# Four graph layers on one core: degrees from one-hot sources ahead of the counts, and the first layer's matmuls beside them

## The reference, cut to what matters

```python
edge_index = jnp.stack([src, dst])
x = _layernorm(x + _L0_gnn_ref(x, edge_index, L0_gnn_W, L0_gnn_b), axis=-1)
...
    # _L0_gnn_ref; ei holds the edges and one more loop at each node
    row, col = (ei[0], ei[1])
    h = jnp.einsum('nd,od->no', x, W) + b
    deg = jnp.zeros((num_nodes,), dtype=h.dtype).at[row].add(1.0)
    deg_inv_sqrt = deg ** (-0.5)
    norm = deg_inv_sqrt[row] * deg_inv_sqrt[col]
    msg = norm[:, None] * h[col]
    out = jax.ops.segment_sum(msg, row, num_segments=num_nodes)
```

## Time and profile before

| | us |
|---|---|
| median of 3 runs | 3709.14 (3701.06 to 3714.17) |
| profiled execution, its own time | 3702.35 |
| its span, first to last instruction | 3700.6 |
| TensorE matmul busy | 3465.3 (94%) |
| VectorE busy | 2024.3 (55%) |
| GpSimd busy | 1349.8 (36%) |
| ScalarE busy | 941.1 (25%) |

### The profile page before, as it was taken

One profiled execution on the slowest core, in us unless ns is written; L12 is line 12 of the kernel. 1 busy time (PEld: TensorE's weight loads), 2 busy tenths in 40 slices (PEclk: granted clock), 3 DMA queues, 4 the chain that ended last, 5 costly groups with the idle time before them and its releaser, 6 DMA issues.

```text
span 3700.6 us, 55568 instructions
## 1 busy us (share of the span) xinstructions
PE 3465.3 (94%) x22684; PEld 2647.9 (72%) x22684; DVE 2024.3 (55%) x4409; ACT 941.1 (25%) x1367; POOL 1349.8 (36%) x1093
## 2 busy tenths in 40 slices
PE   5899678999999999989989989899999999999998
PEld 4666457899899899934434478677777777777797
DVE  7877475432433454364443367777676644444477
ACT  0112123111211312222212266342222122222224
POOL 3777525566456467757777211300000000000021
PEclk8899889999999999989999989999999999999999
DMA  8799884543643455445554355552442322222233
GB/s 288 191 267 290 291 267 112 160 122 81 181 122 99 144 167 173 157 144 163 162 163 136 114 215 177 188 187 98 147 138 79 128 80 81 80 81 66 72 104 107
DMA packets 268704, 557.26 MB, mean 151 GB/s; under 512 B 94954, under 2 KB 118143, under 8 KB 266430
## 3 DMA queue, kind: packets, MB, share of 16 engines
q1 hardware_dynamic: 124504, 384.00, 29.7%
q10 hardware_dynamic: 64520, 116.89, 8.9%
q0 software_dynamic: 79424, 52.83, 8.8%
HBM read 370.13 MB, written 183.44 MB: 150 GB/s over the span
## 4 chain that ended last, share of the span: by engine, by line
PE 76%; DVE 9%; DMA 6%; POOL 5%; issue 3%; ACT 1%; SPq 0%; ACTq 0%; POOLq 0%; DVEq 0%
PE ps L430 52%; PE ps L791 11%; DMA EM<-ee,adr 3%; PE ps L520 3%; PE ps L435 2%; POOL gr L2435 2%; DVE eqj L954 2%; POOL EM L2425 2%; DVE eqj L951 1%; PE ps L676 1%; PE ps L677 1%; PE ps L678 1%; POOL gl L2435 1%; DMA slab<-T 1%; PE ps L444 1%
## 5 line engine op out<-in xcount | busy, mean ns | idle before, releaser
L430 PE MATMUL ps<-a,yy 128*128 128x384 f16 (+5 forms) x3200 | 430.5, 297 | 6.2 <-DVE yy L1627 5.3
L430 PE MATMUL ps<-wb,xh 128*128 128x256 f16 (+1 forms) x2560 | 427.3, 274 | 8.6 <-DVE xl L1199 5.4
L791 PE MATMUL ps<-mh,whl 128*128 128x384 f16 (+5 forms) x2048 | 427.2, 302 | 8.5 <-DVE ml L1774 7.5
L2475 POOL TENSOR_TENSOR graw<-graw,rsb 128x1280 f32<-128x1280 f32 (+1 forms) x2 | 5.7, 2851 | 1090.9 <-DMA graw<-GD 1090.9
L430 PEld LDWEIGHTS ps<-a,yy 128*128 128x128 f16 (+1 forms) x3200 | 312.0, 98 | 124.0 <-DVE yy L1627 5.6
L2386 POOL DMA_INDIRECT TR<-cnt,adr x167 | 268.1, 1605 | 352.5 <-DMA TR<-cnt,adr 325.6
L430 PE MATMUL ps<-wb,xl 128*128 128x256 f16 (+1 forms) x1280 | 350.1, 273 | 0.0
L676 PE MATMUL ps<-sl,x 128*128 128x512 f16 (+1 forms) x800 | 307.5, 384 | 36.9 <-ACT ue L2108 30.3
L2386 POOL DMA_INDIRECT T<-cnt,adr x167 | 265.2, 1588 | 139.9 <-DMA T<-cnt,adr 81.1
L791 PE MATMUL ps<-ml,whl 128*128 128x384 f16 (+5 forms) x1024 | 307.7, 300 | 0.0
L677 PE MATMUL ps<-sl,x 128*128 128x512 f16 (+1 forms) x800 | 307.5, 384 | 0.0
(11 more groups left out here) (346 smaller groups left out, 6908.3 us busy)
## 6 DMA issues: line engine op xcount, KB each, us to landing
TR<-zero_w SPq DMA_DIRECT2D x80, 625.0 KB, 5.3
EM<-neg ACTq DMA_DIRECT2D x40, 625.0 KB
wraw<-in_L_gnn_weight SPq DMA_DIRECT2D x48, 512.0 KB, 3.3
UD<-ue ACTq DMA_DIRECT2D x90, 256.0 KB, 3.1
uu<-UD SPq DMA_DIRECT2D x45, 512.0 KB, 6.1
ar<-TR SPq DMA_DIRECT2D x72, 320.0 KB
eb<-EM SPq DMA_DIRECT2D x9, 2500.0 KB, 9.0
ar<-TR SPq DMA_DIRECT2D x72, 305.0 KB
```

What stands on the lines that cost most here:

```text
L430: i = pe.matmul(ap, l, r, start=(q == 0), stop=(q == len(pairs) - 1))
L791: ins = pe.matmul(ps[:, 0:cn], l, r, start=(q == 0), stop=(q == len(pairs) - 1))
```

## The change

The degrees no longer come from the finished counts. Sources are split on VectorE into 32 a + b, compared with a row 0 to 39 (and 0 to 31) into fp16 one-hot tables `oha` and `ohb`, and 167 matmuls of 32x40 add their products: the number of edges at source 32 a + b. One more matmul spreads these over partitions, and a mask picks each node's. Row sums and diagonals go.

The fold steps are dealt anew: still three behind projections 1 to 8, then two instead of five, and the last 34 (`REST`) behind the projections, in four parts: beside the one-hot tables, around the degree matmuls, before the root, and beside the scaling. Scaling now stands ahead of the slab sums, row tile by row tile. The slabs have six buffers, and the first waits for the degrees.

The first layer's row tiles 0 to 3 take all eight banks at once and are multiplied tile of counts by tile of counts, as `bp` comes in; row tiles 4 to 9 follow as before, with the turned rows behind them by a table. SyncE loads x ahead of the BD writes, and the first pieces of weights behind them.

```diff
-FOLD = [range(3 * n - 3, 3 * n) if 0 < n < 9 else range(24 + 56 * (n - 9) // 11, 24 + 56 * (n - 8) // 11) if n else range(0)
-        for n in range(20)]
+FOLD = [range(3 * n - 3, 3 * n) if 0 < n < 9 else range(2 * n + 6, 2 * n + 8) if n else range(0) for n in range(20)]
+
+REST = [range(46, 58), range(58, 63), range(63, 68), range(68, 80)]
...
-        slab = [at(f"slab{i}", [128, N], F32, O + 72 + 5 * i) for i in range(7)]
+        slab = [at(f"slab{i}", [128, N], F32, O + 80 + 5 * i) for i in range(6)]
...
# tensor
-            rs = [psum.take("rowsum", c, b=5 + c) for c in range(3)]
...
+            for q in REST[0]:
+                fold(q)
+            ps = psum.take("degs", n=5)
+            w.wait_ge(*V("oh"))
+            w.wait_ge(*psum.empty("degs"))
+            for t in range(ET):
+                r = EP if t < E_LAST else EP - 1
+                i = pe.matmul(ps[0:32, 0:40], ohb[0:r, t, :], oha[0:r, t, :], start=(t == 0), stop=(t == ET - 1))
+            i.then_inc(*P.tick("degs"))
+            for q in REST[1]:
+                fold(q)
+            ps = psum.take("dega", n=5)
+            w.wait_ge(*V("dct"))
+            w.wait_ge(*psum.empty("dega"))
+            pe.matmul(ps[:, 0:40], spread[:, :], dct[:, :], start=True, stop=True).then_inc(
+                *P.tick("dega"))
+            for r in REST[2:]:
+                for q in r:
+                    fold(q)
...
+            for k in range(NT):
+                w.wait_ge(*V("bp", k))
+                for i in range(4):
+                    for j in range(2):
+                        w.wait_ge(*V("y", k, j))
+                        if k == 0:
+                            w.wait_ge(*psum.empty("z", i, j))
+                        first_layer(i, j, k)
+            behind_z = {(4, 0): (0,), (4, 1): (1,), (5, 1): (2,), (6, 0): (3,), (7, 0): (4,), (8, 0): (5,), (9, 0): (6,),
+                        (9, 1): (7, 8, 9)}
+            for i in range(4, NT):
...
+                    for m in behind_z.get((i, j), ()):
+                        w.wait_ge(*A("x1", m))
+                        turn_rows("xT", m, zt[m % NX])
# vector
+            for c in range(4):
+                for q in REST[0][3 * c:3 * c + 3]:
+                    low_fold(q)
+                t0, t1 = 42 * c, min(42 * c + 42, ET)
...
+                for to, m, n in ((oha, 1, 40), (ohb, 0, 32)):
+                    dve.tensor_tensor(to[:, t0:t1, :], sab[:, m, t0:t1, None].broadcast_to([EP, t1 - t0, n]),
+                                      step[:, None, 0:n].broadcast_to([EP, t1 - t0, n]), ALU.is_equal).then_inc(*V.tick("oh"))
+            for q in REST[1][:3]:
+                low_fold(q)
+            w.wait_ge(*P("degs"))
...
+            for q in REST[2]:
+                low_fold(q)
+            rsqrt(dve, w, dis[:, :], deg[:, :], t10[:, :], "dis")
+            w.wait_ge(*V("rsqrt", "dis"))
+            more = iter(REST[3])
+            for i in range(NT):
...
+                    for q in [q for _, q in zip(range(1), more)]:
+                        low_fold(q)
# scalar
             for q in range(16 * NFR):
+                if q == REST[3][0]:
+                    root_of(dis[:, :], deg[:, :], V("deg"), "dis")
+                    w.wait_ge(*V("rsqrt", "dis"))
+                if q >= REST[3][0] and q % 2 == 0:
+                    scale_rows((q - REST[3][0]) // 2)
...
+            for i in range(6, NT):
+                scale_rows(i)
             put_fold(2 * NFR - 1)
# sync
                 elif u == 0:
                     w.wait_ge(*P("y", 19))
+                    w.wait_ge(*V("deg"))
...
+            w.wait_ge(*P("fold", 2 * NFR - 1, 1))
+            w.wait_ge(*V("wmx"))
+            for i in range(NX):
+                load_x(i)
             w.wait_ge(*V("bp", 9))
...
-                        w.wait_ge(*(V("deg") if layer == 0 else P("am", 9, 2)))
+                        w.wait_ge(*(V("bp", 9) if layer == 0 else P("am", 9, 2)))
```

More of the change, by code:

```diff
@@ L30 @@
 XS = 1024.0
+WHOLE = 1.5 * 2.0 ** 23
 KB = 1024
@@ L509, in turn_rows, with first_layer @@
                                ident[0:r, 0:r]) for m in range(4)]).then_inc(*P.tick(stage, i, h))
-            for i in range(NT):
+            def first_layer(i, j, k):
                 r = ROWS[i]
-                for j in range(2):
-                    ps = psum.take("z", i, j)
+                ps = psum.at("z", i, j)
+                for q, y in enumerate((yhi, ylo)):
+                    ins = pe.matmul(ps[0:r, :], bp[0:ROWS[k], k, 128 * i:128 * i + r],
+                                    y[0:ROWS[k], k, 512 * j:512 * j + 512], start=(k == 0 and q == 0),
+                                    stop=(k == NT - 1 and q == 1))
+                if k == NT - 1:
+                    ins.then_inc(*P.tick("z", i, j))
@@ new lines, in tensor @@
+            for i in range(4):
+                for j in range(2):
+                    psum.take("z", i, j)
+            for k in range(NT):
+                w.wait_ge(*V("bp", k))
+                for i in range(4):
+                    for j in range(2):
[5 more added lines that the diff above has]
+                        (9, 1): (7, 8, 9)}
@@ L516, in tensor @@
+            for i in range(4, NT):
+                for j in range(2):
+                    psum.take("z", i, j)
                     w.wait_ge(*psum.empty("z", i, j))
                     for k in range(NT):
-                        w.wait_ge(*V("y", k, j))
-                        for q, y in enumerate((yhi, ylo)):
-                            ins = pe.matmul(ps[0:r, :], bp[0:ROWS[k], k, 128 * i:128 * i + r],
-                                            y[0:ROWS[k], k, 512 * j:512 * j + 512], start=(k == 0 and q == 0),
-                                            stop=(k == NT - 1 and q == 1))
@@ L1002, in vector @@
                     equal_keys(1, ts, whole)
-            dve.tensor_copy(onesb[:, :], onesf[:, 0:1].broadcast_to([128, 128])).then_inc(*V.tick("onesb"))
-            dve.memset(deg[:, :], 1.0).then_inc(*V.tick())
+            dve.tensor_reduce(out=own[:, :], in_=ident[:, :].rearrange("p (m b) -> p m b", m=4), axis=AX.X,
+                              op=ALU.add).then_inc(*V.tick())
+            dve.tensor_copy(spread[:, :].rearrange("p (m b) -> p m b", m=4),
+                            ident[0:32, None, 0:32].broadcast_to([32, 4, 32])).then_inc(*V.tick())
@@ new lines, in vector @@
+            dve.tensor_copy(sab[:, 0, :], ei[:, 0, :]).then_inc(*V.tick())
+            w.wait_ge(*V.now())
+            dve.tensor_scalar(out=sab[:, 1, :], in0=sab[:, 0, :], scalar1=-15.5, scalar2=1.0 / 32.0, op0=ALU.add,
+                              op1=ALU.mult).then_inc(*V.tick())
+            w.wait_ge(*V.now())
+            dve.tensor_scalar(out=sab[:, 1, :], in0=sab[:, 1, :], scalar1=WHOLE, scalar2=None, op0=ALU.add).then_inc(*V.tick())
+            w.wait_ge(*V.now())
+            dve.tensor_scalar(out=sab[:, 1, :], in0=sab[:, 1, :], scalar1=WHOLE, scalar2=None, op0=ALU.subtract).then_inc(
+                *V.tick())
@@ new lines, in vector @@
+            w.wait_ge(*V.now())
+            dve.tensor_reduce(out=deg[:, :], in_=dgp[:, :, :], axis=AX.X, op=ALU.add).then_inc(*V.tick())
+            w.wait_ge(*V.now())
+            dve.tensor_scalar(out=deg[:, :], in0=deg[:, :], scalar1=1.0, scalar2=None, op0=ALU.add).then_inc(*V.tick("deg"))
+            for q in REST[2]:
[3 more added lines that the diff above has]
+            more = iter(REST[3])
@@ new lines, in vector @@
+            for i in range(NT):
+                r = ROWS[i]
+                for j in range(2):
+                    c = slice(512 * j, 512 * j + 512)
+                    w.wait_ge(*A("yhi", i, j))
+                    dve.scalar_tensor_tensor(out=ylo[0:r, i, c], in0=yraw[0:r, i, c], scalar=dis[0:r, i:i + 1],
+                                             in1=yhi[0:r, i, c].bitcast(F32), op0=ALU.mult,
+                                             op1=ALU.subtract).then_inc(*V.tick("y", i, j))
+                    for q in [q for _, q in zip(range(1), more)]:
+                        low_fold(q)
@@ L2563, in load_piece_of @@
                         *ww_in[layer][j % 2].tick(j))
-            for i in range(NX):
-                load_x(i)
             load_piece_of(0, 0)
```

117 lines of the change are left out of this document (45 added, 72 removed).

## The result

| | before | after |
|---|---|---|
| median of the runs side by side, us | 3705.25 (7 runs) | 3728.59 (7 runs) |
| span of the profiled execution | 3700.6 | 3722.3 |
| first slab sum starts | 435.58 | 482.84 |
| last slab sum ends | 485.24 | 534.13 |
| last result of the first layer taken | 597.81 | 626.83 |

What follows compares the result with a forecast made beforehand. Bound: TensorE's chain (76%), at 250 to 620 us a queue from counts through slab sums to first layer. +45 before the sums, -5 in them, -22 behind, -2 tail: +16 on 3702.35, 3718; 3725 on the median's scale, range 3699 to 3745.

Steps and rivals of the forecast that it cites:

- Stops before the slabs: TensorE waiting for fold banks: twice 6.6, twice 1.5 of half clock, 2.5 at projection 17; 18.7, projection 19 ending at 388.7.
- premise that five folds a projection leave no such stop: With five folds a projection, VectorE has done the needed split ahead, so TensorE does not stall for a bank.
- unstalled 370.0: End of projection 19 on TensorE from its own work alone, without stalls: projections 75.6, key groups 14.5, folds 27.3.
- One-hot tables and degrees: Before the slabs: comparisons 13.4, ready at 419.5; 167 one-hot matmuls 7.5, done at 433.1; degrees at 441.0.
- hidden wait of the slabs: SyncE's wait for degrees before slab 0 costs nothing: slabs land at 451, VectorE arrives at 480, 29 us of cover.
- First sum: VectorE's first slab sum starts at 480.4 in place of 435.58, 45 later.
- The sums: Ten slab sums at 4.8 a row tile; last ends 44.3 after the first, 49.6 before: -5.
- The first layer behind them: First layer ends 90.2 after the last sum, 112.6 before: -22, with TensorE stops of 15.1 and 4.8 around late weights.
- Tail: Behind the first layer, transposes fill part of the wait for the last row tile, so half clock may stay away: -2.
- Case 1: Rival: folds don't stall, projection 19 ends at 370, first sum at 456.9; 3701 on the median's scale; chance 0.14.
- Case 2: Rival: ww lands within 8 of the last sum, first layer ends at 597.8, only the tail changes; 3707; chance 0.10.
- Case 4: Rival: one-hot matmuls at 0.112 (+11) and slabs at 5.3 with six buffers (+4); 3740; chance 0.17.

Runs made afterwards that it cites:

- c_out: Changed kernel with ScalarE's copy-out of a finished fold group (put_fold) placed ahead of load_fold; first sum 448.34, ratio to the kernel before 1.0006.
- b_seven: Changed kernel with seven slab buffers in place of six, the seventh waiting for the last fold; ratio to the kernel before 1.0125.
- a_pieces: Changed kernel with SyncE's loads of the first two weight pieces (ww) ahead of the ten BD writes; ratio to the kernel before 1.0117.
- f_spread: Changed kernel with the first two weight pieces ahead of the BD writes, those dealt out 4, 3 and 3 behind later pieces; ratio to the kernel before 1.0054.
- all_late: Changed kernel: copy-out before load, two weight pieces before unsplit BD writes, eight slab buffers, four scalings between sums, later weight reductions; ratios to kernel before 0.9892, 0.9933.
- before_c: Kernel before the change, with ScalarE's put_fold placed ahead of load_fold; ratio to the unedited kernel before 1.0001.

## Why the prediction was right, and where it was off

It said 3725 and slower; 3728.59 came. The 3.6 between them flatter it: the median of the kernel before came out 3.9 lower than the one that it started from, so the medians lie 23.3 apart, and the profiled spans 21.7, where the sum had +16.

- **Stops before the slabs: right in kind and place.** Two gaps of 6.6 were foretold ahead of folds 24 and 32, and 6.47 came twice; 2.5 at projection 17, and 2.34 came. Their half clock was undersized: by the comparison with c_out the three cost 22.4, not 18.7, and only 15.3 of it is idle time; behind the first stop nine matmuls ran 0.43 apart and the next projection took 7.30 in place of 6.86. And its premise that five folds a projection leave no such stop was too strong: the kernel before has stops of 2.40 and 2.24 there. Projection 19 ended at 393.3, not 388.7. Its unstalled 370.0 is borne out: c_out needs 117.6 from the start of projection 9, the sum had 117.4.
- **One-hot tables and degrees.** Comparisons ready 4.3 late, all from the projections; 13.4 us for them was right. The 167 matmuls took 4.73, not 7.5. My estimate between rows was too high. The Trainium skill ("TensorE: Matmul & The Clock Gate", Wait — 56ns, not 53.3ns?) has a floor of about 25 ns from start to start, by which the term is an estimated 4.2: the trace, with 28, lies a little above it. Degrees at 443.1 (441.0), hidden wait of the slabs as said.
- **First sum** 482.8 for 480.4: +47.3, not +45.
- **The sums: the step that failed.** "One slab buffer fewer matters little ... then 4.8 each: the last sum ends 44.3 after the first." It was 51.3, and -5 became +1.6. The missing 7.0 are three terms, less 0.7 for a third row tile that came early. The pitch is 5.17, not 4.8: 2.2 over six row tiles (whether six buffers are the reason stays open, by b_seven and the kernels with eight; before, with seven, it was 4.95). The last row tile came 6.9 behind the ninth, not 4.8, and so it did before (475.09 to 481.98): 2.1. And its own operations with a wait took 4.2, where 9.9 for the third tile and seven pitches leave them 0.8 of the 44.3: 3.4. I had carried the steady pitch to the end of the stage and left almost nothing for what follows the last slab.
- **The first layer behind them: right.** 92.7, said 90.2. The stop for ww came with 14.35 (15.1) after one transpose of row tile 0, the second with 4.86 (4.8). The ww landing was foretold at 20.7, and VectorE got it at 21.8 (555.96 less 534.13). a_pieces and f_spread bear out that the place behind BD in the queue makes the pieces late; of the 19.6 us between 92.7 and the 73.1 without that wait, the queue's order alone gives back 9.6, and with the reductions later 14 to 15. The last 5 were not tried; all_late's two traces still have a stop of 6.5 and 6.7 behind a wait for weights.
- **Tail** -2.3, said -2.
- **The rivals.** Case 1 (folds don't stall) was false, but c_out is what it describes: first sum 448.3. It had 456.9; 6.2 of the difference is the stop at 221 us, which it left in, and 3 the one-hot matmuls. Case 2 (weights not late) was false. Case 4's slabs at 5.3 came true in part; its matmuls at 112 ns did not.

At the first layer's end the prediction was 11.9 us low: 2.4 for the first sum, 7.0 in the sums, 2.5 behind them. That the span's rise came within 6 us of it owes something to luck: 6.6 us were given back in the gathers and at the end, where nothing was changed.

## What to carry to other kernels

Work put on an engine ahead of a stage does not only cost its own time: it makes every stop before that stage count, and a stop that was hidden (before_c, 1.0001) becomes the largest item (c_out, 34.5 us). Before giving such a change up, look for an instruction that stands behind another's wait without needing it; here two lines in another order turned a loss of 0.6 to 0.8% into about level (1.0006, interval 0.9971 to 1.0041), and with weights, buffer and scalings moved too into 0.9932. When a long queue of transfers gets less cover, see which of them the next stage wants first; moving one pair ahead only hands the stop to the next pair, and spreading out the transfers in between made another reader of that data (GpSimd) 21 us later.

## What the runs showed of the hardware

167 fp16 matmuls of 40 columns, each with weights of its own, start 28 ns apart (4.73 us in all), far below the 58 ns of the 128-column ones. The 42-tile comparisons with fp16 output (1680 elements in 1.91 us) run at the rate of the fp32 sums (1250 elements in 1.46 us), 1.1 to 1.2 ns an element: against these the narrower output bought nothing. And the kernel before took some 90 to 115 us longer on two chips than on the others, from one stage on, whatever the reason: on these two the gathers took 793 to 840 us from first to last, 737 to 752 on the others, and the 450 us behind them 12 to 34 us more than in the changed kernel's first trace, with the marks before the gathers within 6 us of each other.
